# Relative positions by four row quarters: a matmul of 128 rows and 128 columns becomes four of 32 rows and 32 columns

## What is computed

```python
qkv = x @ qkv_w.T + qkv_b                      # q: [b, head, i, d]
used = rel_emb padded to 2*L-1 distances       # [head, m, d]
logits = einsum('lbhd,hmd->lbhm', q, used)     # unscaled queries
pos[b, h, i, j] = logits[i, b, h, L-1-i+j]     # the shift by i; -1e8 outside the table
probs = softmax(q @ k.T * scale + pos)
```

## Time and profile before

| | |
|---|---|
| median of three runs | 289.87 us |
| profiled execution: its time, its span | 286.78 us, 285.0 us |
| TensorE matmul, busy | 256.7 us, 90% |
| TensorE weight load, busy | 202.1 us, 71% |
| DVE, ACT, POOL busy | 204.1, 213.9, 140.5 us |
| mean granted TensorE clock | 0.983 |
| line 707 in the chain that ended last | 28.78 us |

### The profile page before, as it was taken

One profiled execution on the slowest core, in us unless ns is written; L12 is line 12 of the kernel. 1 busy time (PEld: TensorE's weight loads), 2 busy tenths in 40 slices (PEclk: granted clock), 3 DMA queues, 4 the chain that ended last, 5 costly groups with the idle time before them and its releaser, 6 DMA issues.

```text
span 285.0 us, 5973 instructions
## 1 busy us (share of the span) xinstructions
PE 256.7 (90%) x1912; PEld 202.1 (71%) x1912; DVE 204.1 (72%) x564; ACT 213.9 (75%) x569; POOL 140.5 (49%) x135
## 2 busy tenths in 40 slices
PE   4989999999999998888898669999998999999980
PEld 3679998787787776666665445668786888788850
DVE  2598735877888788889899983589885456845524
ACT  7472651898888887888899778688888887698850
POOL 5018002400111149667542003578998998699970
PEclk9999999999999999999999979999999999999995
DMA  5719310596623316766650001966581796597101
GB/s 122 167 36 409 108 57 2 146 259 230 168 78 88 95 37 134 172 176 179 176 147 3 1 2 37 241 187 179 166 228 37 179 240 181 140 231 199 52 0 37
DMA packets 52243, 37.94 MB, mean 133 GB/s; under 512 B 15794, under 2 KB 43124, under 8 KB 52212
## 3 DMA queue, kind: packets, MB, share of 16 engines
q1 hardware_dynamic: 52212, 37.57, 49.3%
HBM read 30.48 MB, written 7.08 MB: 132 GB/s over the span
## 4 chain that ended last, share of the span: by engine, by line
PE 51%; DVE 16%; POOL 12%; issue 11%; ACT 6%; DMA 1%; POOLq 1%; SPq 0%; DVEq 0%; ACTq 0%
PE bank L723 17%; POOL unit_lo L634 12%; PE bank L707 10%; PE bank L758 6%; ACT probs L979 4%; PE bank L740 4%; PE bank L768 3%; DVE neg_max L1215 3%; DVE probs_t L1222 3%; PE bank L746 2%; PE bank L656 2%; DVE x_tok L1248 2%; PE bank L663 1%; DVE stats L1242 1%; DVE neg_max L1209 1%
## 5 line engine op out<-in xcount | busy, mean ns | idle before, releaser
L634 POOL TENSOR_TENSOR unit_lo<-unit,unit_hi 128x512 fp32r<-128x512 f32 x68 | 86.6, 1294 | 35.6 <-ACT unit_hi L1071 34.4
L979 ACT ACTIVATE probs<-bank,neg_max 128x128 f32<-128x128 f32 x224 | 63.0, 399 | 1.8 <-DVE neg_max L1215 1.6
L1346 DVE SCALAR_TENSOR_TENSOR scaled<-bank,roots 128x512 f32<-128x512 f32 x64 | 43.8, 686 | 28.3 <-PE bank L723 22.4
L1070 ACT ACTIVATE unit<-scaled 128x512 f32<-128x512 f32 x68 | 42.8, 630 | 18.3 <-DVE scaled L1346 17.7
L1215 DVE TENSOR_REDUCE neg_max<-bank 128x4 f32<-128x512 f32 x56 | 38.3, 684 | 12.5 <-PE bank L746 12.5
L758 PE MATMUL bank<-ident,probs 128*128 128x128 f32 x256 | 39.9, 279 | 6.8 <-ACT probs L979 6.7
L1071 ACT ACTIVATE unit_hi<-scaled 128x512 fp32r<-128x512 f32 x68 | 41.9, 617 | 0.0
L758 PEld LDWEIGHTS bank<-ident,probs 128*128 128x128 f32 x256 | 30.1, 141 | 14.9 <-ACT probs L979 12.3
L746 PE MATMUL bank<-k_bd,q_stk 128*128 128x512 f32 x64 | 34.0, 531 | 0.0
L707 PE MATMUL bank<-spread,rel_t 128*128 128x128 f32 x256 | 28.9, 275 | 0.0
L707 PEld LDWEIGHTS bank<-spread,rel_t 128*128 128x128 f32 x256 | 28.7, 192 | 0.1
(11 more groups left out here) (202 smaller groups left out, 475.2 us busy)
## 6 DMA issues: line engine op xcount, KB each, us to landing
roots<-root_dram SPq DMA_DIRECT2D x60, 256.0 KB, 4.6
q_stk<-q_dram SPq DMA_DIRECT2D x16, 128.0 KB, 3.0
k_bd<-k_dram SPq DMA_DIRECT2D x32, 64.0 KB, 2.3
incoming<-in_L_ffn_up_w SPq DMA_DIRECT2D x4, 512.0 KB, 4.7
q_stk<-qc_dram SPq DMA_DIRECT2D x16, 128.0 KB, 3.2
k_bd<-kc_dram SPq DMA_DIRECT2D x32, 64.0 KB, 2.6
incoming<-in_L_ffn_down_w SPq DMA_DIRECT2D x4, 512.0 KB, 4.1
k_dram<-k_hi SPq DMA_DIRECT2D x2, 512.0 KB, 3.4
```

Source lines behind the costliest of these rows:

```text
L634: nc.gpsimd.tensor_tensor(unit_lo[:, k % R], unit[:, k % 3], unit_hi[:, k % R], ALU.subtract).then_inc(lo_ready, 1)
L979: last = nc.scalar.activation(probs[:, U % 3, h4 * L:(h4 + 1) * L], ps[BS[U % 3]][:, h4 * L:(h4 + 1) * L], ACT.Exp, bias=neg_max[:, U % 4, ...
L1070: nc.scalar.activation(unit[:, k % 3], scaled[:, k % 3], ACT.Square)
L1346: ins = nc.vector.scalar_tensor_tensor(scaled[:, k % 3], h, 0.0, roots[:, n % ROOT_RING, c % ROOTS], ALU.max, ALU.mult)
```

## The change

The rows of q_t, rel_t and the queries' bias are ordered in four quarters of 32, each with four heads: row 32f + 4d + x holds channel d of head 4f + x. The keys keep the old order; since queries and keys are gathered from DRAM by the same pattern, SP stores the queries in the old order with four stores of 32 rows for each of the two parts.

A position is now four matmuls, one for each quarter f: 32 rows of rel_t as weights (128 columns), 32 columns of the spread (4 heads x 8 sequences), output in a bank of its own for each quarter. A bank holds 16 positions of one quarter; a block of 16 positions is four tasks, bias{n}_0 to bias{n}_3, whose banks are waited for together at the block's start. The blocks run in the order BLOCKS = 0, 2, 1, 3, 4, 6, 5, 7. By by_vector, blocks 0, 1, 6 and 7 are evicted by DVE, 2 to 5 by ACT, 16 evictions each, of 128 x 512 as before.

The spread has a quarter of the columns: 4 instructions for 32 positions instead of 16, all four chunks stay in the tile, none waits for TensorE, and all stand ahead of DVE's first bias eviction. The bias of queries and keys is turned by two transposes instead of one.

```diff
+TILES = 4
+TROWS, TH = 128 // TILES, H // TILES
+TCOLS = TH * NB
+TI = 512 // TCOLS
+BLOCKS = [n for m in range(L // TI // 4) for n in (m, m + L // TI // 4)]
+BLOCKS += [n + L // TI // 2 for n in BLOCKS]
+
 TASKS = (["w_self", "x0", "x1", "q0", "q1", "rel", "k0", "k1", "v0", "v1", "w_cross", "ctx0", "ctx1",
           "vc0", "vc1", "w_router"]
-         + [f"bias{n}" for n in range(L // 4)]
+         + [f"bias{n}_{f}" for n in BLOCKS for f in range(TILES)]
          + ["kc0", "kc1"])
 
 
 def by_vector(task):
 
     if task.startswith("bias"):
-        i = 4 * int(task[4:])
-        return i < REL0 or i >= MAX_REL
+        i = TI * int(task[4:].split("_")[0])
+        return i < REL0 or i + TI > MAX_REL
...
-        q_spread = spread[:, :].rearrange("p (r i n) -> p r i n", r=2, i=32)
+        q_spread = spread[:, 0:L * TCOLS].rearrange("p (i n) -> p i n", n=TCOLS)
...
+            def keep_queries(part, what):
+
+                rows = q_dram[part].rearrange("(d f x) t -> f d x t", f=TILES, x=TH)
+                for f in range(TILES):
+                    sp.dma_start(rows[f], what[f * TROWS:(f + 1) * TROWS, :]).then_inc(q_kept, 16)
+
             every = slice(0, NB * L)
             sp.wait_ge(q_high, 1)
-            keep(q_dram, (0,), q_hi, every, q_kept)
+            keep_queries(0, q_hi)
...
+            keep_queries(1, q_lo)
...
-            nc.tensor.transpose(ps[5][:, 0:2], qkvb_perm[:, :], ident[0:2, 0:2]).then_inc(bias_col, 1)
+            nc.tensor.transpose(ps[5][:, 0:2], qkvb_perm[:, 0, :], ident[0:2, 0:2])
+            nc.tensor.transpose(ps[5][:, 2:4], qkvb_perm[:, 1, :], ident[0:2, 0:2]).then_inc(bias_col, 1)
...
-            for n in range(L // 4):
-                start(f"bias{n}")
-                if n % 8 == 0:
-                    pe.wait_ge(spread_ready, n // 8 + 1)
-                for m in range(4):
-                    i = 4 * n + m
-                    last = nc.tensor.matmul(bank_of(f"bias{n}")[:, m * 128:(m + 1) * 128],
-                                            rel_t[:, L - 1 - i:2 * L - 1 - i], q_spread[:, i // 32 % 2, i % 32, :],
-                                            start=True, stop=True)
-                last.then_inc(task_done, 1)
+            for n in BLOCKS:
+                for f in range(TILES):
+                    start(f"bias{n}_{f}")
+                pe.wait_ge(spread_ready, TI * n // 32 + 1)
+                for m in range(TI):
+                    i = TI * n + m
+                    for f in range(TILES):
+                        rows = slice(f * TROWS, (f + 1) * TROWS)
+                        ins = nc.tensor.matmul(bank_of(f"bias{n}_{f}")[:, m * TCOLS:(m + 1) * TCOLS],
+                                               rel_t[rows, L - 1 - i:2 * L - 1 - i], q_spread[rows, i, :],
+                                               start=True, stop=True)
+                        if m == TI - 1:
+                            ins.then_inc(task_done, 1)
...
+            for task in TASKS:
+                if task.startswith("bias") and not by_vector(task):
+                    n, f = (int(a) for a in task[4:].split("_"))
+                    nc.scalar.copy(pos[:, f * TCOLS:(f + 1) * TCOLS, TI * n:TI * (n + 1)],
+                                   done(task).rearrange("p (i r) -> p r i", i=TI)).then_inc(out_a, 1)
...
+            def by_tile(ap, rows):
+                return ap.rearrange("p (f d x) -> p f x d" if rows else "p (f x d) -> p f x d", f=TILES, x=TH)
...
+            turned = done("w_self")
+            nc.vector.tensor_copy(by_tile(w_t[:, 0, :], True), by_tile(turned[:, 0:D], False))
...
-                if c >= 2:
-                    dve.wait_ge(task_done, TASKS.index(f"bias{8 * (c - 1) - 1}") + 1)
                 src = q_t[:, 32 * NB * c:32 * NB * (c + 1)].rearrange("p (i b) -> p i b", b=NB)
-                for h in range(H):
-                    last = nc.vector.tensor_scalar(q_spread[:, c % 2, :, h * NB:(h + 1) * NB], src,
-                                                   head_mask[:, h:h + 1], None, ALU.mult)
+                for x in range(TH):
+                    last = nc.vector.tensor_scalar(q_spread[:, 32 * c:32 * (c + 1), x * NB:(x + 1) * NB], src,
+                                                   head_mask[:, x:x + 1], None, ALU.mult)
...
-            def bias_out(n):
-                nc.vector.tensor_tensor(pos[:, :, 4 * n:4 * n + 4], done(f"bias{n}").rearrange("p (i r) -> p r i", i=4),
-                                        rel_mask[:, 4 * n:4 * n + 4].unsqueeze(1).broadcast_to([128, H * NB, 4]),
+            def bias_out(task):
+                n, f = (int(a) for a in task[4:].split("_"))
+                cols = slice(TI * n, TI * (n + 1))
+                nc.vector.tensor_tensor(pos[:, f * TCOLS:(f + 1) * TCOLS, cols],
+                                        done(task).rearrange("p (i r) -> p r i", i=TI),
+                                        rel_mask[:, cols].unsqueeze(1).broadcast_to([128, TCOLS, TI]),
...
+            dve.wait_ge(out_a, out_count("q1", False))
+            spread_queries(2)
+            spread_queries(3)
             dve.wait_ge(masks_made, 1)
-            for n in range(L // 4):
-                if n == 7:
-                    dve.wait_ge(out_a, out_count("q1", False))
-                if n in (7, 16):
-                    spread_queries(2 + (n > 8))
-                if by_vector(f"bias{n}"):
-                    bias_out(n)
+            for task in TASKS:
+                if task.startswith("bias") and by_vector(task):
+                    bias_out(task)
```

More of the change, by code:

```diff
@@ L220, in decoder_layer @@
         identb = sb("identb", [128, 128], BF16)
-        head_mask = sb("head_mask", [128, H])
+        head_mask = sb("head_mask", [128, TH])
         rel_mask = sb("rel_mask", [128, L])
@@ L230, in decoder_layer @@
         qkvb_raw = sb("qkvb_raw", [2, D])
-        qkvb_perm = sb("qkvb_perm", [2, D])
-        qkvb_col = sb("qkvb_col", [128, 2])
+        qkvb_perm = sb("qkvb_perm", [2, 2, D])
+        qkvb_col = sb("qkvb_col", [128, 4])
         kb_col = sb("kb_col", [128, 1])
@@ L478, in _ @@
             sp.wait_ge(q_split, 1)
-            keep(q_dram, (1,), q_lo, every, q_kept)
+            keep_queries(1, q_lo)
             sp.wait_ge(k_split, 1)
             keep(k_dram, (2, 3), k_t, every, k_kept)
-            sp.wait_ge(q_kept, 16 * 2)
+            sp.wait_ge(q_kept, 16 * 2 * TILES)
             sp.wait_ge(k_kept, 16 * REPS)
@@ L571, in _ @@
                 .then_inc(consts_made, 1)
-            pool.wait_ge(spread_ready, 2)
+            pool.wait_ge(spread_ready, 4)
             pool.wait_ge(q_high, 1)
@@ L584, in _ @@
                                     pb_row[:, :].unsqueeze(1).broadcast_to([128, NB, D]), ALU.add).then_inc(xb_made, 1)
-            pool.wait_ge(task_done, TASKS.index(f"bias{L // 4 - 1}") + 1)
+            pool.wait_ge(task_done, TASKS.index("kc0"))
             nc.gpsimd.memset(k_bd2[:, :, :, :].bitcast(F32), 0.0).then_inc(zeroed, 1)
@@ L598, in _ @@
                     if b == 0:
-                        pool.wait_ge(q_kept, 16 * 2)
+                        pool.wait_ge(q_kept, 16 * 2 * TILES)
                     nc.gpsimd.tensor_copy(q_hi[:, cols].bitcast(F32R), q_t[:, cols]).then_inc(qc_split, 1)
@@ L939, in _ @@
             act.wait_ge(bias_col, 1)
-            link(nc.scalar.copy(qkvb_col[:, :], ps[5][:, 0:2]))
+            link(nc.scalar.copy(qkvb_col[:, :], ps[5][:, 0:4]))
             nc.scalar.activation(q_t[:, 0:HT], done("q0"), ACT.Identity, bias=qkvb_col[:, 0:1]).then_inc(out_a, 1)
             nc.scalar.activation(q_t[:, HT:], done("q1"), ACT.Identity, bias=qkvb_col[:, 0:1]).then_inc(out_a, 1)
-            link(nc.scalar.mul(kb_col[:, :], qkvb_col[:, 1:2], SCALE))
+            link(nc.scalar.mul(kb_col[:, :], qkvb_col[:, 3:4], SCALE))
             for f in range(2):
@@ L961, in _ @@
             nc.scalar.copy(k_hi[:, :].bitcast(F32R), k_t[:, :]).then_inc(k_high, 1)
-            for n in range(L // 4):
-                if not by_vector(f"bias{n}"):
-                    nc.scalar.copy(pos[:, :, 4 * n:4 * n + 4],
-                                   done(f"bias{n}").rearrange("p (i r) -> p r i", i=4)).then_inc(out_a, 1)
+            for task in TASKS:
[3 more added lines that the diff above has]
+                                   done(task).rearrange("p (i r) -> p r i", i=TI)).then_inc(out_a, 1)
             act.wait_ge(k_kept, 16 * REPS)
@@ L1141, in _ @@
             dve.wait_ge(ident_made, 1)
-            nc.vector.tensor_reduce(head_mask[:, :], ident[:, :].rearrange("p (d h) -> p h d", h=H), AX.X, ALU.add).then_inc(heads_made, 1)
+            nc.vector.tensor_reduce(head_mask[:, :], ident[:, :].rearrange("p (n x) -> p x n", x=TH), AX.X, ALU.add).then_inc(heads_made, 1)
+            def by_tile(ap, rows):
+                return ap.rearrange("p (f d x) -> p f x d" if rows else "p (f x d) -> p f x d", f=TILES, x=TH)
             dve.wait_ge(ld["qkvb"], 16)
```

(13 more changed lines are left out.)

## The result

The changed kernel takes 322.38 us (median of four runs, 321.5 to 323.27) against 289.68 us before, a ratio of 1.1158 with a 95% interval of 1.1107 to 1.1209: 32.7 us slower. I had forecast 298.2 us and a range up to 306, so the time lies outside it.

A forecast was written before the change was run, and what follows sets the result against it. The prediction took TensorE alone to bound the relative-position stage. Its terms, 0 + 6.8 + 1.3 + 0.2 = +8.3 us, added to the median of 289.87, gave 298.2 us, with a range from 277 to 306.

The forecast's parts named there:

- term 1: Relative-position matmul stage: four row quarters overlap, loads included, so it takes 28.7 us as now; change 0 us.
- The clock falls: Rival: waits of 1 us and short matmuls count as rest, the stage doubles at half clock: 327 us, chance 0.08.
- The pace at full clock: Relative-position stage: 128-column loads set the pace, quarters load side by side, a block of 16 positions takes 3.6 us.
- Loads one after another: Rival: the quarters' weight loads in the stage do not overlap, +84 + 8.3, 382 us, chance 0.12.
- a slower pace with overlap: Rival: quarters overlap but pairs issue slower or a tile can't load while streaming: 304 to 305 us, chance 0.13.
- Quick quarters: Rival: a tile's load is short, or its columns set the pace: 283.7 or 277.1 us, chance 0.19.
- The bank waits: At 7 block boundaries TensorE stands still for one eviction, 1.04 us (DVE) or 0.93 us (ACT): +6.8 us.
- The end of the stage: After the last matmul four DVE evictions are left, so the first score transpose starts 2.9 us later, for 1.56: +1.3.
- The lead-in: Before the stage there is one small transpose more, 0.19 us on the chain: +0.2.
- What was costed at nothing: DVE's spread falling from 18.4 to about 4.6 us and SP's eight query stores, among others, stay off the chain.

The follow-up runs named there:

- e4: The kernel before, its 128-row relative-position matmuls streaming only the first 32 of 128 columns, no waits added: 312.38 us, ratio 1.0818.
- e1: The changed kernel, but every quarter matmul streams 128 columns instead of 32: 300.29 us, ratio 1.0361 to the kernel before.
- e3: The kernel before, with TensorE waiting ahead of every fourth bank for the eviction of the one just finished: 295.73 us, ratio 1.0242.
- e8: The changed kernel, still streaming 32 columns, with the fourth quarter five positions behind so no bank is waited for: 314.76 us, ratio 1.0905 to the kernel before.
- e6: The changed kernel with the quarter matmuls' operands exchanged: 32 spread columns as weights, 128 columns of rel_t streaming: 291.93 us, ratio 1.0128 to the kernel before.
- e7: The kernel before, with twelve unread matmuls filling TensorE's 3.15 us pause near the end of the attention: 288.37 us, ratio 0.9997.
- e5: The changed kernel with 128 streamed columns and the fourth quarter five positions behind, so no bank is waited for: 293.59 us, ratio 1.0176 to the kernel before.

## Why the prediction was wrong

**The step that failed** is term 1, "0 us", and with it the rival "The clock falls", to which I gave a chance of 0.08. The stage took the price of the lower clock: 22.9 us in the blocks and 1.9 in kc0 and kc1, 24.8 of 32.7. I argued from TensorE's busy share: 2.83 of 5 us with the clock at 1.00 seemed to show that a stage with short waits was safe. The share was the wrong number. In the changed kernel it is 5.00 of 5 us at clock 0.50, since a record of 32 columns still lasts 381 ns in the mean and the next starts 30 to 55 ns after it (3.78 and 7.06 us for 128), so they overlap and fill the time whatever they stream. e4 shows that short streams are enough and e1 that full streams undo the long fall; e3 shows that waits of this kind alone do not make it, e8 that it needs none. The Trainium skill ("TensorE: Matmul & The Clock Gate", Part 1: The HAM clock gate (the "warmup" mystery)) names the two levels and says that the chip sets them by how busy TensorE has been; the trace agrees on the levels, 1.00 and 0.50, and disagrees if "busy" is read as the busy time of a profile.

**The pace at full clock** was right. The first block takes 3.78 us with its fill and its last result, for 3.6 forecast without them, and all but one of e1's blocks take as long. So line 815 was the right row: row quarters load side by side, and eight loads of 128 columns in four quarters take as long as two. "Loads one after another" and "a slower pace with overlap" are out. "Quick quarters" is out: e6, with loads of 32 columns, is what that would have needed. (Its price has a small slip: two loads of 54 ns are 0.108 us a position and 13.8 us, not 14.3. Nothing rests on it.)

**The bank waits** were forecast at 6.8 us in all; alone in e3 they cost 6.6 us. In the changed kernel they measure 6.1 on the chain and 1.5 in the ends of the blocks, 7.6 in all. One wait was forecast at 1.04 or 0.93 us, of which 0.16 (until the last result is out) are part of the block's 3.78 us on the chain; so it is 0.88 and 0.77 against the measured 0.95 and 0.82. That part of the mechanism was right.

**The end of the stage,** +1.3, did not come, because kc0 and kc1 at half clock (3.59 us) cover the four evictions. At full clock (e1) it is +0.8. **The lead-in,** +0.2, was 0.7 in this execution; the profiles of the other runs start the stage between 18.3 and 20.0 us, so I take nothing from it.

**What was costed at nothing** cost nothing: the spread fell off DVE's list and no wait for it appears, and the eight stores of the queries did not show on the chain.

The rival itself was priced at 327 us, the whole stage at half clock, and the time came out at 322.4. Its 28.8 us for the doubled stage were 22.9, since the first block ran at full clock and the ends of blocks are no part of the doubling; the 1.3 at the end was hidden, and the 1.9 of kc0 and kc1 stood in no term.

## What to carry to other kernels

In this kernel tiles of 32 rows did not make the matmul cheaper while its weights were still 128 columns wide: the load set the pace (3.78 us a block, with 32 streamed columns or 128), so the narrow operand has to be the weights before tiles can pay, and banks, evictions and instructions have to keep up then. Read the granted clock beside the busy share: this stage lost half of TensorE's clock at a busy share of 100%, with 32 or 64 columns streamed for each load of 128, and streaming 128, three quarters of them useless, in the shadow of the loads won 22 us. But raise the clock only where TensorE sets the pace (e7).

## What the hardware showed that I had not expected

- Streaming 128 columns where 32 are needed made the kernel 22 us faster (300.3 for 322.4).
- TensorE's clock at 0.50 for 58 us while it was busy for 4.1 to 5.0 of every 5 us, until matmuls of 512 columns had run.
- Short pauses that dropped the clock in one pattern and not in another: seven of 0.70 to 0.87 us, 3.8 us apart, did nothing (e3); two of 0.82 and 0.86 us, 0.90 us apart, brought 3.4 us at half clock (e1).
- Row quarters load their weights side by side: a block of 16 positions with 128 loads of 128 columns in 3.78 us, 30 ns a load, where a single one takes about 0.11 us.
- With 32-column weights and 128-column streams a block of 128 records takes 1.91 us, 15 ns each, half of the fourfold overlap's 3.78, not a quarter.
- Gaps of 0.45 to 2.33 us that no semaphore ends, in e1, e5 and e6, all of which issue small matmuls at full clock; none in e8 at half clock. All eight end 1.32 to 1.49 us after a packet of the instruction queue has landed.
